# A perceiver block on one core: in its first cross-attention the tile maxima are turned by a transposing transfer, and the second pass follows the value product

## The reference, cut to what matters

```python
def _L0_xattn_ref(x, context, ln_gamma, ln_beta, w_q, w_kv, w_out, b_out, gate):
    xn = _layernorm(x, ln_gamma, ln_beta)
    q = (xn @ w_q).reshape(B, SQ, NUM_HEADS, DIM_HEAD)
    kv = context @ w_kv
    k, v = jnp.split(kv, 2, axis=-1)
    ...
    scores = jnp.einsum('bqhd,bkhd->bhqk', q * SCALE, k)
    attn = jax.nn.softmax(scores, axis=-1)
    out = jnp.einsum('bhqk,bkhd->bqhd', attn, v).reshape(B, SQ, INNER)
    out = out @ w_out + b_out
    return out * jnp.tanh(gate[0])
```

## Time and profile before

| | us |
|---|---|
| median of 3 runs | 1178.44 (1177.39 to 1178.67) |
| profiled execution | 1177.7 |
| its span, first to last instruction | 1176.0 |
| TensorE busy | 1142.3 (97%) |
| VectorE busy | 902.3 (77%) |
| ScalarE busy | 901.7 (77%) |
| GpSimd busy | 584.9 (50%) |

### The profile page before, as it was taken

One profiled execution on the slowest core, in us unless ns is written; L12 is line 12 of the kernel. 1 busy time (PEld: TensorE's weight loads), 2 busy tenths in 40 slices (PEclk: granted clock), 3 DMA queues, 4 the chain that ended last, 5 costly groups with the idle time before them and its releaser, 6 DMA issues.

```text
span 1176.0 us, 32589 instructions
## 1 busy us (share of the span) xinstructions
PE 1142.3 (97%) x12775; PEld 816.4 (69%) x12775; DVE 902.3 (77%) x1713; ACT 901.7 (77%) x1551; POOL 584.9 (50%) x548
## 2 busy tenths in 40 slices
PE   8999999999999999999999999999998899889998
PEld 6566666666666666666666666666666758767898
DVE  7777878888888888888878787878774699788632
ACT  5699989888888989898888888888884368686010
POOL 5355656565656665665666565656564070043000
PEclk9999999999999999999999999999999999999999
DMA  6465544445354545354535454544433994150384
GB/s 220 100 191 149 152 117 116 127 96 153 88 158 94 151 93 157 90 154 96 154 88 143 108 136 110 139 108 96 119 89 113 367 352 142 41 180 1 108 284 176
DMA packets 141142, 163.31 MB, mean 139 GB/s; under 512 B 18320, under 2 KB 127280, under 8 KB 140992
## 3 DMA queue, kind: packets, MB, share of 16 engines
q1 hardware_dynamic: 139904, 157.20, 48.0%
q10 hardware_dynamic: 1088, 4.06, 0.9%
HBM read 71.60 MB, written 12.99 MB: 72 GB/s over the span
## 4 chain that ended last, share of the span: by engine, by line
PE 86%; DVE 7%; issue 2%; ACT 2%; DMA 1%; SPq 1%; POOL 0%; DVEq 0%; ACTq 0%; POOLq 0%
PE ps L900 21%; PE ps L872 21%; PE ps L938 7%; PE ps L914 7%; PE ps L2344 4%; PE ps L957 4%; PE ps L955 4%; PE ps L956 4%; PE ps L1669 3%; PE ps L1108 2%; PE ps L2352 2%; PE ps L2126 2%; PE ps L2108 1%; DMA k_st<-k_rest 1%; PE ps L923 1%
## 5 line engine op out<-in xcount | busy, mean ns | idle before, releaser
L468 POOL TENSOR_TENSOR pT_lo<-p_exp,pT_hi 128x896 f16<-128x896 f32 x223 | 421.1, 1888 | 313.5 <-ACT pT_hi L580 313.5
L561 ACT ACTIVATE p_exp<-ps,ln_k,esc 128x896 f32<-128x896 f32 x224 | 246.4, 1100 | 54.2 <-PE ps L938 46.9
L697 DVE TENSOR_REDUCE tile_max<-ps 128x128 f16<-128x896 f32 x224 | 244.4, 1091 | 49.5 <-PE ps L914 47.2
L580 ACT ACTIVATE pT_hi<-p_exp 128x896 f16<-128x896 f32 x224 | 211.9, 946 | 1.0
L692 DVE TENSOR_TENSOR v_lo<-ps,v_hi 128x512 f16<-128x512 f32 x196 | 135.4, 691 | 69.0 <-ACT v_hi L553 66.7
L956 PE MATMUL ps<-v_lo,pT_hi 128*128 128x64 f16 x1568 | 164.4, 193 | 0.0
L955 PE MATMUL ps<-v_hi,pT_hi 128*128 128x65 f16 x1568 | 164.3, 193 | 0.1
L957 PE MATMUL ps<-v_hi,pT_lo 128*128 128x65 f16 x1568 | 163.8, 193 | 0.0
L900 PE MATMUL ps<-c_hi,wk_hi 128*128 128x448 f16 x448 | 158.5, 354 | 1.0 <-DVE k_rest L712 0.6
L900 PE MATMUL ps<-c_hi,wk_lo 128*128 128x448 f16 x448 | 157.9, 352 | 0.0
L900 PE MATMUL ps<-c_lo,wk_hi 128*128 128x448 f16 x448 | 157.9, 352 | 0.0
(11 more groups left out here) (402 smaller groups left out, 2095.5 us busy)
## 6 DMA issues: line engine op xcount, KB each, us to landing
k_st<-k_top SPq DMA_DIRECT2D x444, 112.0 KB, 2.3
k_st<-k_rest SPq DMA_DIRECT2D x444, 56.0 KB, 2.0
xa_cn<-in_ctx SPq DMA_DIRECT2D x14, 896.0 KB, 7.4
me_w<-in_me_w SPq DMA_DIRECT2D x8, 1536.0 KB, 6.3
c_raw<-in_ctxT SPq DMA_DIRECT2D x13, 896.0 KB, 5.7
ctx_parts<-c_hi SPq DMA_DIRECT2D x14, 448.0 KB, 3.5
ctx_parts<-c_lo SPq DMA_DIRECT2D x14, 448.0 KB, 2.8
me_w<-in_me_w SPq DMA_DIRECT2D x8, 768.0 KB, 6.0
```

The costliest lines, as they stand in the source:

```text
L468: nc.gpsimd.tensor_tensor(pT_lo[:, n % 2, :, :].rearrange("p t s -> p (t s)"), p_exp[:, n % 2, :], pT_hi[:, n % 2, :, :].rearrange("p t s ...
L561: nc.scalar.activation(p_exp[:, n % 2, :], s_scores[n % 2], ACT.Exp, bias=ln_k[:, 0:1], scale=esc[:, n // H0 % 2:n // H0 % 2 + 1]).then_in ...
L580: nc.scalar.activation(pT_hi[:, n % 2, :, :].rearrange("p t s -> p (t s)"), p_exp[:, n % 2, :], ACT.Copy).then_inc(pT_hi_ready, 1)
L697: nc.vector.tensor_reduce(tile_max[:, n % 2, :], s_scores[n % 2].rearrange("p (t s) -> p s t", s=S), AX.X, ALU.max).then_inc(tile_max_done, 1)
```

## The change

The turn leaves TensorE. SyncE issues a transposing transfer from `tile_max` to a new SBUF tile `max_by_query`; it waits for the tile maximum first. In its loop the turn of head n + 2 stands ahead of all else of step n, `place_keys` too; the first two turns lie between the prologue's `place_keys`. `new_max` reads `max_by_query` and waits for the transfer (16 counts each). On VectorE `v_low` now stands ahead of `new_max`. On TensorE `lay_max` stands behind `weigh`, and where the step has a value product, or half of one, the second pass stands behind it.

```diff
+        max_by_query = t("max_by_query", [P, 2, S], F16)
...
-        def s_turned(n):
...
+            def turn_max(n):
+                sp.wait_ge(tile_max_done, n + 1)
+                sp.dma_start(max_by_query[:, n % 2, :].rearrange("p (o s) -> p o s", o=1), tile_max[:, n % 2, :], transpose=True).then_inc(max_turned, 16)
+
             for U in range(K_DIRECT, K_AHEAD):
                 place_keys(U)
+                if U == 2 or U == 4:
+                    turn_max(U // 2 - 1)
 
             for n in range(NT):
                 c, h = n // H0, n % H0
+                if n + 2 < NT:
+                    turn_max(n + 2)
...
-                v.wait_ge(max_turned, n + 1)
+                v.wait_ge(max_turned, 16 * (n + 1))
...
-                nc.vector.tensor_scalar(turned[:, i, :], s_turned(n), 1.0, -BIG if c == 0 else m_floor[:, h:h + 1], ALU.mult, ALU.max,
+                nc.vector.tensor_scalar(turned[:, i, :], max_by_query[:, i, :], 1.0, -BIG if c == 0 else m_floor[:, h:h + 1], ALU.mult, ALU.max,
...
             for n in range(NT):
                 c, h = n // H0, n % H0
+                if n and v_at(n - 1):
+                    v_low(*v_at(n - 1))
                 if n + 1 < NT:
                     new_max(n + 1)
-                if n and v_at(n - 1):
-                    v_low(*v_at(n - 1))
...
-            def turn_max(n):
-                pe.wait_ge(tile_max_done, n + 1)
-                if n > 2:
-                    first, f = (n - 2) % 4 == 0, (n - 2) // 4
-                    at_least(pe, flushed, 2 * (f - 1 if first else f))
-                nc.tensor.matmul(s_turned(n), tile_max[:, n % 2, :], ident16[:, :], start=True, stop=True, skip_group_check=True).then_inc(max_turned, 1)
...
-                    turn_max(0)
...
-                if n + 1 < NT:
-                    turn_max(n + 1)
...
-                if n + 1 < NT:
-                    lay_max(n + 1)
...
                 if n:
                     weigh(n - 1)
                 if n + 1 < NT:
+                    lay_max(n + 1)
+                if n + 1 < NT and not v_parts(n):
                     second_pass(n + 1)
...
                     v_project(*at, parts)
+                    second_pass(n + 1)
```

## The result

The changed kernel takes 1411.99 us (median of 4 runs, 1405.83 to 1413.21), the kernel before beside it 1178.56: a ratio of 1.197, 95% interval 1.195 to 1.199, slower. The profiled execution has a span of 1411.2 us against 1176.0, 235.2 more. In the changed kernel's profile `turn_max` is L371, `first_pass` L914, `lay_max` L921, `second_pass` L931, weigh L948 to L950, `place_keys` L362 and L367; `v_project` L872, `new_max` L706 and the lines of ScalarE and VectorE named here are as before.

The account below looks back on a forecast made before the run. TensorE was taken to bound the loop at 61.1 us a chunk; a serial ring would make it 76.4. Thirteen chunks' 199 us, pieces 15, sums 7 and the last chunk made 234 more: 1412 us, range 1370 to 1500.

Parts of the forecast that it names:

- The main step: Loop steps with a whole value product: 4.69 us each after the change, against 3.95 before.
- the ring: Exponent, v_high, v_low, new_max, lay_max, value product, second pass, next exponent in a row, none overlapping: 4.69 us a step.
- Slices in the ring: Four c_high slices a chunk, between an exponent and a v_high on ScalarE, now add 0.55 us each.
- Half steps: Steps at heads 0 and 8, with half a value product: 4.69 less 0.64 us each.
- The landing: Turning transfer, from issue to landed: 2.6 us, with ends 1.4 and 4.6; it decides the steps at heads 1 and 9.
- The pieces and sums: Ternary layer's weight pieces, four a chunk in six chunks, 15 us; 12 sums in the first two chunks, 7 us.
- costs nothing: SyncE's loads, saves and key placing queued behind its wait for the tile maximum: room enough, cost nothing.
- The last chunk: Last chunk: 7.6 us more for its first half, 5 for the second, which has no value products.
- The rival in which it falls throughout: TensorE's clock falls to 1.2 GHz because it idles: 430 us more, 1840 us; chance 0.03.
- The landing as a bound: Rival: transfer's landing sets every step, from L (landing time) = 3.24 us; 1675 us at 4.6; chance 0.15.
- five issues of 0.63: SyncE's issuing in a step: 3.15 us, less than any step's 4.05, so no delay.
- the present price: new_max reading SBUF instead of PSUM on VectorE: left at its 0.35 us.

Follow-up runs that it names:

- The order alone: Kernel before, turn still on TensorE, with only the second pass moved behind the value product: 1291.29 us, ratio 1.096.
- the kernel with weigh in the ring: Kernel before, turn on TensorE, second pass behind the product and v_low ahead of new_max, lay_max still ahead of weigh: 1463.63 us, ratio 1.243.
- The halves: Changed kernel with each chunk's 896 KB context load issued by SyncE as two 448 KB transfers, at heads 8 and 9: 1391.97 us, ratio 1.181.
- the transfer alone: Kernel before with the turn as SyncE's transfer, TensorE's and VectorE's order kept as before: 1373.19 us, ratio 1.166.

## Why the prediction was right

The forecast was 1412 and the measured time is 1411.99. That closeness is partly luck; point by point:

- **The main step held.** The second pass behind the product closes a ring. It was set at 4.69 us; the timeline has 4.58 to 4.62. The order alone shows it without a transfer (4.26 measured, 4.25 summed), and the kernel with weigh in the ring lengthens it by as much as weigh takes (5.22 against 5.24 summed). The differences: `v_low` passes to the next VectorE instruction in 0.60, not 0.72, and the other terms are within 0.02.
- **Slices in the ring held.** 5.14 us behind c_high, 0.52 to 0.56 more, as summed. Half steps: 4.06 at head 8, forecast 4.05.
- **The landing was set too high.** The transfer landed after 2.3 us in the median, not 2.6, so steps 1 and 9 are 3.83 us and not 4.05, and there is no flush to pay for (4.62 at steps 2 and 10 of chunk 12). By these and the shorter ring, a chunk without a load came out at 74.6 us against 76.4 in the sum, and the same chunk takes 61.3 before, not 61.1: 13.3 more and not 15.3, which is 26 us too much in 13 chunks.
- **The pieces and sums were set too high.** The forecast had 15 and 7 us for them. The pieces make 2.3 us a chunk in the order alone (70.8 in chunks 2 to 7, 68.5 in 8 to 11), near the 2.5 forecast. In chunks 0 and 1, where the sums lie, the changed kernel takes 7.9 us more than in two chunks like chunk 12, but the kernel before takes 5.4 more there itself (step 10 left aside in both). In all, chunks 0 to 11 without their step 10 grew by some 10 us more than twelve times what chunk 12 did: 12 less than forecast.
- **A term was missing.** The sum had SyncE's other transfers as "costs nothing", by counting issues alone. The turn issued one step behind the context load lands two microseconds late, TensorE idles, and in 8 of 12 chunks its clock falls: step 10 of chunks 1 to 11 is 86.6 us in all against 11 x 4.62 = 50.8, so 35.8 us. Against what step 10 took before, and with chunk 0, it is 35. The halves gave back 20 us.
- These errors, some 26 and 12 us one way and 35 us and a longer tail (below) the other, nearly cancel. That the total came out at 1412 is luck; the ring, its length and the steps that it sets are not. The last chunk is 65.1 against 53.2, 11.9 more, forecast 12.6.
- **The clock.** The rival in which it falls throughout did not come about (0.98 to 1.00 in the loop), but it does fall at places: behind the context load, and at the loop's end, where TensorE was busy for 6.86 of 10 us:

```profile
1112.00:1122.00 10.00, 6.86 (x80) 5.75 (x81) 4.50 (x12) 5.30 (x9) 3.96 (x3) 0.58 0.03 7
```

From the last exponent on, the work takes 285.6 us against 280.3, about 5 more; the granted clock is 0.51 from 1127 to 1134 us. In the order alone, whose granted clock is 1.00 throughout, it is 280.3 as before.

- **The landing as a bound.** The rival had L = 3.24 as its point in whole steps. The landing was over that in 23 of the 224 turns, 12 of them behind the load; the other 11 lie in seven chunks, 8 of them with an issue of over 1.4 us. Taken out of the new order, though, the transfer by itself costs 196 us: the two costs (114 for the order, 196 for the transfer) overlap, and 233 is less than their sum because the ring through the product gives the transfer most of the time it needs.
- **Issue.** I had five issues of 0.63; the transposing one takes 1.12. With the four others a step needs 3.65 us of SyncE's time, under the changed kernel's steps. Even so 39 turns were issued over 0.3 us late there. Right ahead of them stands a single plain issue of 1.2 to 2.2 us, or a load or a save as one issue more. Counting issues at 0.63 did not show that.
- TensorE's turns, 13.4 us, brought nothing, as forecast: TensorE waits 33 us in every 200.
- `new_max` from SBUF takes 0.34 us, from PSUM 0.35: the present price was the right one.

The Trainium skill ("VectorE: DVE Perf Modes", The three transpose paths) gives 1309 ns for such a transfer; here 2.3 us pass from issue to landing, of which 1.1 are the issue. The Trainium skill's advice in the same page (Rules for kernel authors), TensorE where a PSUM destination will do, is borne out: the transfer alone costs 196 us, and the turns on TensorE take 13.4. That transposing transfers are as fast as ordinary ones (the Trainium skill, "Advanced Engine Details and Errata", X-Bar Transpose) holds roughly for the landing, 2.3 us for 32 KB beside 2.0 for a copy of 56 KB, in the changed kernel as in the earlier trace rows. It doesn't hold for the issue, 1.12 us beside 0.63.

None of these kernels is faster than the one before.

## What to carry to other kernels

When work is moved on one engine, write down for each buffer who empties it and what stands ahead of that in the emptying engine's program: here one moved pass put an exponent, and with it every slice that follows an exponent, between a product and its own bank. Add up such a ring and compare it with the busy engine's own work in a step; if it is longer, the difference is paid every step, and savings on the busy engine are worth nothing. A transfer put on a path of dependences has to be priced with the large transfers in flight beside it, not by its median alone, and changing the queue of the large one doesn't help.

## What the runs showed of the hardware

- A transposing transfer of 32 KB within SBUF is issued in 1.12 us (median; a plain copy 0.63) and lands in 2.2 to 2.3 us, up to 4.6 behind 896 KB from DRAM, and up to 7.9 where that load comes from another engine's queue right ahead of it. It is cut small: packets under 512 bytes rose from 18320 to 54160 in the execution, 160 a transfer.
- Some issues of it took 1.5 to 2.5 us with no load about (L371 at 2.08 in the transfer alone). Single plain issues took 1.2 to 2.2 us at times. What holds them is not settled.
- Behind 2.12 us of idle time TensorE's granted clock fell to 0.50 from about 414 to 417 us, and the product there took 2.51 us instead of 1.29; the idle time thus cost 3.3. The same fall came behind 8 of the 12 context loads.
